# Rotary remainder products on half of the array's rows, an even and an odd key tile side by side, with three score banks

## The chip, the cores and the metric

The kernel runs on one core of one Trainium2 chip. The metric is device time in microseconds, the median of three runs. The profiled execution is a single run with its own time.

## The reference

One transformer layer over 2048 tokens of width 512. The part that matters here is the latent attention with 16 heads, a query of 128 plain and 64 rotary dimensions per head, and one rotary key that all heads share:

```python
cq = rms_norm(x @ w_qa.T, q_a_ln_w)
q = (cq @ w_qb.T)                       # 16 heads x (128 plain + 64 rotary)
ckv = x @ w_kva.T                       # 128 latent + 64 rotary
k_pe = rotate(ckv[..., 128:])           # one rotary key for all heads
ckv_l = rms_norm(ckv[..., :128], kv_a_ln_w)
scores = (q_nope . k_nope + q_pe . k_pe) * scale, causal mask, softmax
out = softmax @ v, then @ w_o.T
x1 = layernorm(x + out);  result = layernorm(x1 + x1 @ (w * s).T + bias)
```

Everything is float32. The kernel folds the key and value up-projections into the queries and into the output projection, so keys and values are both the 128-wide latent row of a token (plus the 64 rotary dimensions for the scores).

## The kernel before, in words

Three phases stand one behind the other, and each engine's instructions are in a fixed order.

The prepare phase (up to about 160 us) projects the tokens, turns the results so that the feature dimension lies on partitions, and writes each as two fp32r tensors, a rounded part ("hi") and the remainder ("lo"). `token_places` (line 412) names the places. The rotary key has 64 dimensions; its rotated row is made twice, so that `key_pe` holds the same 64 rows on partitions 0 to 63 and on 64 to 127, with a hi part (index 0) and a lo part (index 1). `lo(t)` (line 508) makes the lo parts on the vector engine.

The attention phase (about 160 to 1725 us) runs over 64 iterations: 4 groups of 4 heads, and in each the 16 query tiles of 128 tokens, two by two (a pair `s` is two iterations). Iteration `it` works on query tile `tile_of(it)` and takes that number plus one key tiles; there are 544 (iteration, key tile) steps in all. `key_tile(it, t)` (line 603) says which key tile step `t` takes: the diagonal one first, then 0, 1, 2 and so on. For each step:

- `scores` (line 1146) does five matmuls of 128 rows and 512 columns (4 heads by 128 queries) into one PSUM bank: hi key by hi query, hi key by lo query, lo key by hi query for the latent part, then two for the rotary part. `q_pe` holds the hi part of the rotary query on partitions 0 to 63 and its lo part on 64 to 127, so the fourth matmul (hi rotary key on both halves) gives both hi by hi and hi by lo, and the fifth (lo rotary key on both halves) gives lo by hi and lo by lo.
- the scalar engine copies the bank into a ring of 24 slots (`copy_scores`, line 1265), the vector engine keeps the running maximum (`max_of`, line 1426; `masked`, line 1414, for the diagonal tile), and that frees the bank: there are two banks for scores, `N_SCORES = 2`.
- six or more steps later come: subtract the maximum (vector), exp (scalar), rounding to hi (scalar), remainder (GpSimd), the running sum (vector), and `values` (line 1187), three matmuls of 512 columns.

Other work of the tensor engine stands between them: the projection of the queries (`project_q`, `project_pe`), turning and spreading of maxima and sums (`turn_max`, `spread_max`, `turn_sum`, `spread_sum`), and the output projection (`project_out`). Six kinds of these share a set of three auxiliary banks, `N_AUX = 3`: a use waits (`shared`, line 1108) until the reader of the use three before it is done.

The order of all this is written by `plan` (line 817) from a `timetable` (line 658) of slots and phases, with `waits_for` (line 721) saying what must stand ahead of a step. The reader of a use (for `spread_sum` it is `normalise` and the two halves of the output rounding) is put into phase `READ` of the next slot, unless an auxiliary bank is wanted earlier. The phases of a slot are, in order, SPREAD, SCORES_AT, COPIES, SHIFT, EXP, ROUND, VALUES, READ, MAX, USE_AT.

The rotary part of the queries goes through DRAM to change its layout: `store_pe` writes it, and `load_pe` (line 1049) fetches it with four DMAs on SyncE's queue into `q_pe`, one for each of (hi, lo) by (first, second half of the 64 dimensions). The first score step of a pair waits for them ahead of its fourth matmul.

The last phase (from about 1725 us) is the feed-forward layer; the change does not touch it. On the tensor engine the preparation begins with 16 transposes of 128 rows (line 302) and 4 of 64 rows (line 304):

```python
for k in range(KH):
    for o in range(4):
        pe.transpose(m.bank[k][...], wa_rows[:, o, k * P:k * P + P], m.ident[:, :])
for k in range(KH):
    mm = pe.transpose(m.bank[4][...], wa_tail[0:DR, k * P:k * P + P], m.ident[0:DR, 0:DR])
mm.then_inc(wa_turned, 1)
```

Of the kernel before, what the change touches and what calls it, by code (L numbers as in the profile page):

```python
# [8 lines left out]
F32R = mybir.dt.float32r  # L9
BF16 = mybir.dt.bfloat16  # L10
ALU = mybir.AluOpType
# [3 lines left out]
P = 128  # L15
S = 2048
# [4 lines left out]
DN, DR, DV = 128, 64, 128  # L21
DQ = DN + DR
HALF = DR // 2
# [7 lines left out]
HG = H // G  # L31
# [7 lines left out]
def chunk(c):  # L39

    return (c + 1) % NCH


def stored(view):

    return view.bitcast(F32)
# [7 lines left out]
class Memory:  # L54


    def __init__(self, nc, ctx):
        def sb(name, shape, dt=F32):
            return ctx.enter_context(nc.sbuf_tensor(name, shape, dt))

        self.bank = [ctx.enter_context(nc.psum_tensor(f"bank{n}", [P, 512], F32)) for n in range(4, 8)]

        self.rows = ctx.enter_context(nc.psum_tensor("rows", [P, 4 * 512], F32))
        self.bank = [self.rows[:, 512 * n:512 * n + 512] for n in range(4)] + [b[:, :] for b in self.bank]

        self.key_c = sb("key_c", [P, 2, S], F32R)
        self.key_pe = sb("key_pe", [P, 2, S], F32R)
        self.val = sb("val", [P, 2, NT, C], F32R)
        self.cq = sb("cq", [P, 2, KR, 512], F32R)
        self.wq = sb("wq", [P, 2, KR, WCOL], F32R)  # L70
        self.wo = sb("wo", [P, 2, HG, HID], F32R)
        self.ident = sb("ident", [P, P])
        self.ident16 = sb("ident16", [P, P], BF16)
        self.mask16 = sb("mask16", [P, P], BF16)
        self.table = sb("table", [P, 2, 4 * P])
        self.small = sb("small", [P, 64])

        self.pool = sb("pool", [P, RING * 512])

        self.cq_dram = nc.dram_tensor("cq_dram", (NCH, P, 2 * KR * 512), F32, kind="Internal").ap()  # L80
        self.wq_dram = nc.dram_tensor("wq_dram", (G, P, 2 * KR * WCOL), F32, kind="Internal").ap()
        self.wo_dram = nc.dram_tensor("wo_dram", (G, P, 2 * HG * HID), F32, kind="Internal").ap()

        self.turned_tables = self.pool[:, 0:8 * P].rearrange("p (w n) -> p w n", n=P)
        self.table_dram = nc.dram_tensor("table_dram", (4, P, 8, P), F32, kind="Internal").ap()
        self.pe_dram = nc.dram_tensor("pe_dram", (G * NT // 2, 2, 2, P, 2 * P), F32, kind="Internal").ap()
        self.table_copied = ctx.enter_context(nc.semaphore("table_copied"))
        self.table_stored = ctx.enter_context(nc.semaphore("table_stored"))
        self.y_stored = ctx.enter_context(nc.semaphore("y_stored"))

        self.wo_free = ctx.enter_context(nc.semaphore("wo_free"))
        self.cq_free = ctx.enter_context(nc.semaphore("cq_free"))

        self.ffn_w_loaded = ctx.enter_context(nc.semaphore("ffn_w_loaded"))
        self.y_first_loaded = ctx.enter_context(nc.semaphore("y_first_loaded"))
        self.y_dram = nc.dram_tensor("y_dram", (NT, P, HID), F32, kind="Internal").ap()


def prepare_phase(nc, m, x, w_qa, w_kva, w_qb, w_kvb, w_o, q_ln, kv_ln, ident_in, mask_in, cos_in, sin_in):
# [6 lines left out]
    with ExitStack() as ctx:  # L106
# [3 lines left out]
        at = 0  # L110
# [56 lines left out]
        tok_lo = sem("tok_lo")  # L167
# [244 lines left out]
        def token_places(c, t):  # L412

            yield (TR[:, 0:QLR].rearrange("p (k n) -> p k n", k=KR), lambda a: m.cq[:, a, :, t * P:t * P + P], None)
            yield TR[:, QLR:QLR + C], lambda a: m.key_c[:, a, bass.ds(chunk(c) * 512 + t * P, P)], kv_w
            yield KT, lambda a: m.key_pe[:, a, bass.ds(chunk(c) * 512 + t * P, P)], None

        @block.scalar
        def _(act):
# [67 lines left out]
        def _(dve):  # L487
# [12 lines left out]
            with dve.Fori(0, NCH) as c:  # L500
# [7 lines left out]
                def lo(t):  # L508

                    for n, (src, dst, scale) in enumerate(token_places(c, t)):  # L510
                        dve.wait_ge(tok_hi, c * 12 + 3 * t + max(n, 1) + 1)
                        if scale is None:
                            nc.vector.tensor_tensor(dst(1), src, stored(dst(0)), ALU.subtract).then_inc(tok_lo, 1)
                        else:
                            nc.vector.scalar_tensor_tensor(out=dst(1), in0=src, scalar=scale, in1=stored(dst(0)),
                                                           op0=ALU.mult, op1=ALU.subtract).then_inc(tok_lo, 1)
# [43 lines left out]
N_TILE = G * NT * (NT + 1) // 2  # L560
N_PAIR = N_ITER // 2
LEAD = 6
N_SCORES, N_AUX = 2, 3
Y_FIRST = 10


# [23 lines left out]
def tile_of(it):  # L590

    return 2 * pair_of(it // 2) + 1 - it % 2
# [5 lines left out]
def keys(it):  # L598

    return tile_of(it) + 1  # L600


def key_tile(it, t):

    return tile_of(it) if t == 0 else t - 1


FIRST = [sum(keys(n) for n in range(it)) for it in range(N_ITER + 1)]
# [3 lines left out]
def number(it, t):  # L612

    return FIRST[it] + t
# [95 lines left out]
def previous(it, t, back):  # L710

    n = number(it, t) - back
    return TILES[n] if n >= 0 else None
# [7 lines left out]
def waits_for(step):  # L721

    what, it, *rest = step
    if what == "scores":
# [2 lines left out]
            yield ("q_lo", it // 2, j)  # L727
        if number(it, *rest) >= N_SCORES:
            yield ("max", *previous(it, *rest, N_SCORES))
    elif what == "max":  # L730
        yield ("scores", it, *rest)
        if number(it, *rest) >= RING:
# [84 lines left out]
def plan():  # L817

    order, given, uses = [], set(), []

    def give(step):

        if step in given:
            return
        given.add(step)
        for before in waits_for(step):
            give(before)
        if step[0] in AUX_USES:
            if len(uses) >= N_AUX:
                for reader in readers(uses[-N_AUX]):  # L830
                    give(reader)
            uses.append(step)
        order.append(step)

    at = {}
    for n, phase, step in timetable():
        at.setdefault((n, phase), []).append(step)
        for reader in readers(step):
            at.setdefault((n + 1, READ), []).append(reader)
    for key in sorted(at):  # L840
        for step in at[key]:
            give(step)
    return order, uses
# [25 lines left out]
def attention_phase(nc, m, w_ffn, scale_w):  # L869


    with ExitStack() as ctx:
        def sb(name, shape, dt=F32):
            return ctx.enter_context(nc.sbuf_tensor(name, shape, dt))
# [4 lines left out]
        ring = m.pool[:, :].rearrange("p (r n) -> p r n", r=RING)  # L879
        q_c = sb("q_c", [P, 2, HG, 512], F32R)  # L880
        q_pe = sb("q_pe", [P, HG, 512], F32R)
        split_p = sb("split_p", [P, 2, 2, 512], F32R)
        o_t = sb("o_t", [P, 2, 512], F32R)
        o_sum = sb("o_sum", [P, 2, 512])
# [60 lines left out]
        def by_head(view):  # L945

            return view.rearrange("p (h n) -> p h n", h=HG)
# [21 lines left out]
        def q_slot(it):  # L969

            return (it // 2 % 2) * 2 * P + tile_of(it) % 2 * P
# [17 lines left out]
        def _(sp):  # L989
# [59 lines left out]
            def load_pe(s):  # L1049
                at = pair_slot(s)  # L1050
                sp.wait_ge(pe_stored, 32 * (s + 1))
                if s:
                    sp.wait_ge(pe_loaded, 64 * s)
                if s >= 2:

                    sp.wait_ge(scores_ready, finished(2 * s - 3))
                for x in range(2):
                    for e in range(2):
                        row = DR * x + HALF * e
                        sp.dma_start(stored(q_pe[row:row + HALF, :, at:at + 2 * P]),  # L1060
                                     m.pe_dram[s, x, e].rearrange("(h d) n -> d h n", h=HG)).then_inc(pe_loaded, 16)
                if s == 1:
                    store_tables()
                if s == 2:
                    sp.wait_ge(m.table_stored, 64)
                if MADE <= s + 2 < N_PAIR:
                    load_table(s + 2)
# [24 lines left out]
        def _(pe):  # L1092
# [53 lines left out]
            def scores(it, t):  # L1146
                n, j, at = number(it, t), key_tile(it, t), q_slot(it)
                if t == 0:

                    if it % 2 == 0:  # L1150
                        pe.wait_ge(q_lo, q_count(it // 2, PAIRS - 1))
                if n >= N_SCORES:

                    pe.wait_ge(scores_maxed, n - N_SCORES + 1)
                out = SCORES[n % N_SCORES]
                k_c, k_pe = m.key_c[:, :, j * P:j * P + P], m.key_pe[:, :, j * P:j * P + P]
                terms = [(k_c[:, 0], q_c[:, 0, :, at:at + P]), (k_c[:, 0], q_c[:, 1, :, at:at + P]),
                         (k_c[:, 1], q_c[:, 0, :, at:at + P]), (k_pe[:, 0], q_pe[:, :, at:at + P]),
                         (k_pe[:, 1], q_pe[:, :, at:at + P])]
                for z, (k, q) in enumerate(terms):  # L1160
                    if z == 3 and t == 0 and it % 2 == 0:
                        pe.wait_ge(pe_loaded, 64 * (it // 2 + 1))
                    mm = pe.matmul(by_head(out), k, q, start=(z == 0), stop=(z == 4))  # L1163
                mm.then_inc(scores_ready, 1)

            def turn_max(it):
                u = ("turn_max", it)
# [619 lines left out]
```

## Time and profile before

| | |
|---|---|
| median of 3 runs | 1812.79 us (1812.04 to 1815.03) |
| the profiled execution | 1809.61 us, of which the span of its instructions is 1807.6 us |
| tensor engine, matmuls | 1704.4 us busy, 94% |
| tensor engine, weight loads | 1391.9 us busy, 77% |
| vector engine | 1401.4 us, 78% |
| scalar engine | 1095.1 us, 61% |
| GpSimd | 972.5 us, 54% |
| DMA | 94 GB/s on average |

Busy time is the union of an engine's instructions. A matmul's duration in the trace contains the time until its last results are through, and the next begins before that; so the distance from start to start says what a matmul occupies, not its duration. A weight load overlaps the matmul ahead of it. "Idle before" is time in which the engine did nothing ahead of an instruction, and the name behind the arrow is what ended it.

### The profile page before, as it was taken

Reading aid. Unit: us, or ns where it says so; the run is one execution under the profiler, and the core shown is the slowest. Engines: PE = TensorE matmul, PEld = TensorE weight load, DVE = VectorE, ACT = ScalarE, POOL = GpSimd, SP = SyncE. Lnnn points to the kernel's source line nnn. Section 1 sums busy time; section 2 is a strip of 40 time slices with the busy share of each in tenths; the row PEclk is TensorE's granted clock in tenths of the full one; section 3 lists DMA queues with packets and bytes.
Section 4 is the critical chain, followed back from the end, with each engine's and each line's share of the span. In section 5 each row is a group of like instructions: output and inputs, shape, how many; then the busy total and the mean of one; then the engine's idle time right before and its main releaser. Section 6 shows DMA issues by size and latency. Waiting matters only on the chain. (4 is left out here: it accounts for less than half of the span.)

```text
span 1807.6 us, 27750 instructions
## 1 busy us (share of the span) xinstructions
PE 1704.4 (94%) x8729; PEld 1391.9 (77%) x8729; DVE 1401.4 (78%) x2531; ACT 1095.1 (61%) x2088; POOL 972.5 (54%) x883
## 2 busy tenths in 40 slices
PE   5997899999999899999999999999999999998586
PEld 3665778888888788888888788888888888886432
DVE  1555578888888688888888688888888888888376
ACT  2553367667666567676666576766667766676310
POOL 2321245556555456655555455655655666566555
PEclk9998999999999999999999999999999999999899
DMA  7785412112322221213231322212222211111411
GB/s 241 280 328 224 131 58 82 59 60 76 117 71 82 88 88 38 81 58 117 71 99 36 123 65 77 65 59 98 66 71 88 65 59 59 56 45 30 141 63 58
DMA packets 109960, 170.52 MB, mean 94 GB/s; under 512 B 12992, under 2 KB 83648, under 8 KB 107456
## 3 DMA queue, kind: packets, MB, share of 16 engines
q1 hardware_dynamic: 100992, 121.14, 21.1%
q0 software_dynamic: 7104, 23.60, 4.0%
q10 hardware_dynamic: 1728, 24.12, 3.2%
q8 instruction: 67, 1.10, 0.3%
q14 instruction: 69, 0.57, 0.1%
HBM read 104.86 MB, written 68.16 MB: 96 GB/s over the span
## 5 line engine op out<-in xcount | busy, mean ns | idle before, releaser
L1342 POOL TENSOR_TENSOR split_p<-pool,split_p 128x512 fp32r<-128x512 f32 x544 | 702.6, 1294 | 509.6 <-ACT split_p L1287 509.3
L1163 PE MATMUL rows<-q_c,key_c 128*128 128x512 f32 x1632 | 475.9, 400 | 2.8 <-DVE top L1433 1.6
L1275 ACT COPY pool<-rows 128x512 f32<-128x512 f32 x480 | 281.8, 587 | 236.6 <-PE rows L1163 235.8
L1433 DVE TENSOR_TENSOR top<-rows,top 128x512 f32<-128x512 f32 x420 | 288.8, 688 | 137.4 <-ACT pool L1275 134.3
L1448 DVE TENSOR_TENSOR pool<-bank,pool 128x512 f32<-128x512 f32 x544 | 369.8, 680 | 20.5 <-PE bank L1183 20.5
L1280 ACT ACTIVATE pool<-pool 128x512 f32<-128x512 f32 x544 | 346.0, 636 | 16.0 <-DVE pool L1448 15.2
L1287 ACT CAST split_p<-pool 128x512 fp32r<-128x512 f32 x544 | 333.3, 613 | 14.8 <-PE bank L1196 14.8
L1163 PE MATMUL rows<-q_pe,key_pe 128*128 128x512 f32 x1088 | 337.0, 391 | 3.2 <-DMA q_pe<-pe_dram 3.2
L1460 DVE TENSOR_TENSOR bank<-bank,pool 128x512 f32<-128x512 f32 x480 | 331.0, 690 | 0.1
L1163 PEld LDWEIGHTS rows<-q_c,key_c 128*128 128x128 f32 x1632 | 288.9, 189 | 50.1 <-DVE top L1433 3.1
L1163 PEld LDWEIGHTS rows<-q_pe,key_pe 128*128 128x128 f32 x1088 | 204.2, 188 | 48.8 <-DMA q_pe<-pe_dram 3.6
L1196 PE MATMUL bank<-split_p,val 128*128 128x512 f32 x544 | 214.0, 393 | 5.0 <-POOL split_p L1342 4.7
L1193 PE MATMUL bank<-split_p,val 128*128 128x512 f32 x544 | 214.2, 394 | 3.1 <-ACT o_sum L1293 2.9
L1194 PE MATMUL bank<-split_p,val 128*128 128x512 f32 x544 | 212.2, 390 | 0.0
L1226 PE MATMUL rows<-wo,o_t 128*128 128x512 f32 x528 | 131.2, 398 | 9.6 <-issue 8.7
L1347 POOL TENSOR_TENSOR o_t<-o_sum,o_t 128x512 fp32r<-128x512 f32 x64 | 83.0, 1296 | 84.2 <-ACT o_t L1305 83.9
L1196 PEld LDWEIGHTS bank<-split_p,val 128*128 128x128 f32 x544 | 102.1, 188 | 32.9 <-POOL split_p L1342 11.4
L1226 PEld LDWEIGHTS rows<-wo,o_t 128*128 128x128 f32 x528 | 101.5, 193 | 32.6 <-issue 11.1
L1193 PEld LDWEIGHTS bank<-split_p,val 128*128 128x128 f32 x544 | 102.1, 188 | 28.5 <-ACT o_sum L1293 5.6
L1194 PEld LDWEIGHTS bank<-split_p,val 128*128 128x128 f32 x544 | 102.2, 188 | 21.2
L1305 ACT CAST o_t<-o_sum 128x512 fp32r<-128x512 f32 x64 | 39.7, 620 | 119.8 <-DVE o_sum L1472 94.0
L1128 PE MATMUL rows<-cq,wq 128*128 128x256 f32 x792 | 104.9, 287 | 0.0
(158 smaller groups left out, 2066.2 us busy)
## 6 DMA issues: line engine op xcount, KB each, us to landing
cq<-cq_dram SPq DMA_DIRECT2D x30, 768.0 KB, 5.0
y<-y_dram SPq DMA_DIRECT2D x64, 256.0 KB, 3.0
q_pe<-pe_dram SPq DMA_DIRECT2D x128, 128.0 KB, 2.7
y_dram<-y SPq DMA_DIRECT2D x64, 256.0 KB, 2.0
wq_dram<-wq ACTq DMA_DIRECT2D x4, 2304.0 KB, 11.7
wo_dram<-wo ACTq DMA_DIRECT2D x4, 2048.0 KB, 10.5
pe_dram<-by_sin SPq DMA_DIRECT2D x32, 256.0 KB, 2.1
pe_dram<-by_cos SPq DMA_DIRECT2D x32, 256.0 KB, 2.2
```

The lines of the kernel that those rows point to most:

```text
L1163: mm = pe.matmul(by_head(out), k, q, start=(z == 0), stop=(z == 4))
L1193: pe.matmul(OUT, m.val[:, 0, j, :], split_p[:, n % 2, 0, :], start=(t == 0), stop=False)
L1194: pe.matmul(OUT, m.val[:, 1, j, :], split_p[:, n % 2, 0, :], start=False, stop=False)
L1196: pe.matmul(OUT, m.val[:, 0, j, :], split_p[:, n % 2, 1, :], start=False, stop=(t == keys(it) - 1)).then_inc(values_done, 1)
L1226: mm = pe.matmul(aux(u), o_t[:, a, h * P:h * P + P], m.wo[:, b, h, :], start=(n == 0), stop=(n == 3 * HG - 1))
L1275: nc.scalar.copy(slot(n), SCORES[n % N_SCORES]).then_inc(scores_copied, 1)
L1280: nc.scalar.activation(slot(n), slot(n), ACT.Exp).then_inc(exp_done, 1)
L1287: nc.scalar.copy(split_p[:, n % 2, 0, :], slot(n)).then_inc(p_hi, 1)
L1342: nc.gpsimd.tensor_tensor(split_p[:, n % 2, 1, :], slot(n), stored(split_p[:, n % 2, 0, :]), ALU.subtract).then_inc(p_lo, 1)
L1433: nc.vector.tensor_tensor(out, SCORES[n % N_SCORES], slot(number(it, 0)) if t == 1 else out, ALU.max).then_inc(scores_maxed, 1)
L1448: nc.vector.tensor_tensor(slot(n), MAXES, slot(n), ALU.add).then_inc(shifted, 1)
L1460: nc.vector.tensor_tensor(TOTAL, TOTAL, slot(n), ALU.add).then_inc(summed, 1)
```

## The change

The lo part of the rotary key is no longer held twice. A new tensor `key_pe_lo` of half the width holds even key tiles on partitions 0 to 63 and odd ones on 64 to 127. The fifth matmul of a score step now has 64 rows: lo key by hi query, without the lo by lo product. Odd key tiles need the hi query on partitions 64 to 127, in a new tensor `q_pe_hi` that `load_pe` fills with two more DMAs.

Key tiles are taken in an order in which an even and an odd one follow each other. The first step of such a couple "opens" it: it does its four matmuls of 128 rows, its own 64-row matmul, and directly behind that the 64-row matmul of its partner, as the first product in the partner's bank. The partner, one step later, adds its four matmuls of 128 rows. Query tiles with an even number take their diagonal tile alone. There are three score banks and two auxiliary ones, and `normalise` stands in phase EXP of its slot in place of READ.

```diff
-        self.key_pe = sb("key_pe", [P, 2, S], F32R)
+        self.key_pe = sb("key_pe", [P, S], F32R)
+        self.key_pe_lo = sb("key_pe_lo", [P, S // 2], F32R)
...
-            yield KT, lambda a: m.key_pe[:, a, bass.ds(chunk(c) * 512 + t * P, P)], None
+            yield KT, lambda a: m.key_pe[:, bass.ds(chunk(c) * 512 + t * P, P)], None
...
+                        if n == 2:
+                            rows = slice(DR * (t % 2), DR * (t % 2) + DR)
+                            nc.vector.tensor_tensor(m.key_pe_lo[rows, bass.ds(chunk(c) * 2 * P + t // 2 * P, P)], src[rows],
+                                                    stored(dst(0))[rows], ALU.subtract).then_inc(tok_lo, 1)
...
-N_SCORES, N_AUX = 2, 3
+N_SCORES, N_AUX = 3, 2
...
-    return tile_of(it) if t == 0 else t - 1
+    i = tile_of(it)
+    if t < 1 + i % 2:
+        return i - t
+    return t - 1 - i % 2
+def opens_couple(it, t):
+    return (tile_of(it) + t) % 2 == 1 and t + 1 < keys(it)
+def closes_couple(it, t):
+    return t > 0 and opens_couple(it, t - 1)
...
+        if opens_couple(it, *rest) and number(it, *rest) >= N_SCORES - 1:
+            yield ("max", *previous(it, *rest, N_SCORES - 1))
...
-            at.setdefault((n + 1, READ), []).append(reader)
+            at.setdefault((n + 1, EXP if reader[0] == "normalise" else READ), []).append(reader)
...
-                    sp.wait_ge(pe_loaded, 64 * s)
+                    sp.wait_ge(pe_loaded, 96 * s)
...
+                for e in range(2):
+                    row = DR + HALF * e
+                    sp.dma_start(stored(q_pe_hi[row:row + HALF, :, at:at + 2 * P]),
+                                 m.pe_dram[s, 0, e].rearrange("(h d) n -> d h n", h=HG)).then_inc(pe_loaded, 16)
...
-                if n >= N_SCORES:
+                if n >= N_SCORES and not closes_couple(it, t):
                     pe.wait_ge(scores_maxed, n - N_SCORES + 1)
...
+                if closes_couple(it, t):
+                    for z, (k, q) in enumerate(whole):
+                        mm = pe.matmul(by_head(out), k, q, start=False, stop=(z == 3))
+                    mm.then_inc(scores_ready, 1)
+                    return
+                for z, (k, q) in enumerate(whole):
                     if z == 3 and t == 0 and it % 2 == 0:
-                        pe.wait_ge(pe_loaded, 64 * (it // 2 + 1))
-                    mm = pe.matmul(by_head(out), k, q, start=(z == 0), stop=(z == 4))
-                mm.then_inc(scores_ready, 1)
+                        pe.wait_ge(pe_loaded, 96 * (it // 2 + 1))
+                    pe.matmul(by_head(out), k, q, start=(z == 0), stop=False)
+                half_row(it, t, start=False, stop=True).then_inc(scores_ready, 1)
+                if opens_couple(it, t):
+                    if n + 1 >= N_SCORES:
+                        pe.wait_ge(scores_maxed, n + 1 - N_SCORES + 1)
+                    half_row(it, t + 1, start=True, stop=False)
+            def half_row(it, t, start, stop):
+                j, at = key_tile(it, t), q_slot(it)
+                rows = slice(DR * (j % 2), DR * (j % 2) + DR)
+                q = q_pe_hi if j % 2 else q_pe
+                return pe.matmul(by_head(SCORES[number(it, t) % N_SCORES]), m.key_pe_lo[rows, j // 2 * P:j // 2 * P + P],
+                                 q[rows, :, at:at + P], start=start, stop=stop)
```

## Rows read from the trace of the kernel before

**Rows 1.** Stages by windows: window, length, then each engine's busy us, clock, DMA

```profile
core 0: us, PE busy (x) PEld busy (x) DVE busy (x) ACT busy (x) POOL busy (x), PEclk, DMA share, GB/s
500.00:700.00 200.00, 195.32 (x1027) 165.89 (x1026) 161.46 (x274) 128.85 (x240) 111.88 (x91) 0.98 0.25 80
700.00:900.00 200.00, 199.73 (x1054) 170.10 (x1053) 168.62 (x284) 134.37 (x250) 116.59 (x94) 1.00 0.24 77
900.00:1100.00 200.00, 195.11 (x1027) 165.22 (x1026) 161.58 (x275) 129.77 (x242) 112.87 (x93) 0.99 0.23 75
```

**Rows 2.** Waits of the weight loads, 190 to 1725 us: total us, times, longest

```profile
PEld bank L1196 <- POOL split_p L1342: 11.4, 16, 1.1
...
PEld bank L1193 <- ACT o_sum L1293: 5.6, 7, 1.3
...
PEld rows L1163 <- DVE top L1433: 3.1, 4, 1.6
```

**Rows 3.** Groups by line and form: shapes, count, busy us, mean ns, idle before

```profile
L1163 PE MATMUL rows<-q_c,key_c 128*128 128x512 f32 x1632 | 475.9, 400 | 2.8 <-DVE top L1433 1.6 <-DVE pool L1422 1.2
L1163 PE MATMUL rows<-q_pe,key_pe 128*128 128x512 f32 x1088 | 337.0, 391 | 3.2 <-DMA q_pe<-pe_dram 3.2
```

**Rows 4.** Timeline of matmuls around 906 us: start us, us, engine, line, count

```profile
905.98 0.39 PE L1193 MATMUL bank<-split_p,val 128*128 128x512 f32 x1
906.20 0.39 PE L1194 MATMUL bank<-split_p,val 128*128 128x512 f32 x1
906.43 0.39 PE L1196 MATMUL bank<-split_p,val 128*128 128x512 f32 x1
906.66 0.84 PE L1163 MATMUL rows<-q_c,key_c 128*128 128x512 f32 x3
907.34 0.62 PE L1163 MATMUL rows<-q_pe,key_pe 128*128 128x512 f32 x2
```

**Rows 5.** Timeline of the weight loads of the same stretch

```profile
905.98 0.19 PEld L1194 LDWEIGHTS bank<-split_p,val 128*128 128x128 f32 x1
906.21 0.19 PEld L1196 LDWEIGHTS bank<-split_p,val 128*128 128x128 f32 x1
```

**Rows 6.** Timeline of the vector engine, one step and the next

```profile
907.08 0.68 DVE L1433 TENSOR_TENSOR top<-rows,top 128x512 f32<-128x512 f32 x1
907.67 0.68 DVE L1448 TENSOR_TENSOR pool<-bank,pool 128x512 f32<-128x512 f32 x1
908.27 0.69 DVE L1460 TENSOR_TENSOR bank<-bank,pool 128x512 f32<-128x512 f32 x1
908.87 0.68 DVE L1433 TENSOR_TENSOR top<-rows,top 128x512 f32<-128x512 f32 x1
```

**Rows 7.** Durations at line 1163 (rotary part), ns min/median/max, first and last start

```profile
L1163 PE MATMUL rows<-q_pe,key_pe x1088: 387/389/497, 184.4 to 1644.9; 128*128 128x512 f32 x182
```

**Rows 8.** Timeline of matmuls at the start: from 128-row to 64-row transposes

```profile
18.35 1.27 PE L302 MATMUL rows<-ident,wa_rows 128*128 128x128 f32 x5
19.55 0.69 PE L304 MATMUL bank<-ident,wa_tail 64*128 64x64 f32 x4
```

**Rows 9.** Timeline of the weight loads of the same stretch

```profile
18.99 0.23 PEld L302 LDWEIGHTS rows<-ident,wa_rows 128*128 128x128 f32 x1
19.55 0.39 PEld L304 LDWEIGHTS bank<-ident,wa_tail 64*128 64x128 f32 x3 [0.33 <-issue]
```

**Rows 10.** Durations of the matmuls at line 302

```profile
L302 PE MATMUL rows<-ident,wa_rows x16: 421/421/474, 15.9 to 19.2; 128*128 128x128 f32 x16
```

**Rows 11.** Timeline: four 128-column transposes later in the kernel

```profile
908.47 0.60 PE L1212 MATMUL rows<-ident,sums 128*128 128x128 f32 x4
```

**Rows 12.** The rotary queries' loads: durations of the issue, and when they were waited for

```profile
L1060 SPq DMA_DIRECT2D q_pe<-pe_dram x128: 303/432/1684, 177.8 to 1619.2; - x128
...
195.22 0.73 PE L1163 MATMUL rows<-q_pe,key_pe 128*128 128x512 f32 x2 [3.17 <-DMA q_pe<-pe_dram]
```

More of the change, by code:

```diff
@@ L511, in lo @@
                         dve.wait_ge(tok_hi, c * 12 + 3 * t + max(n, 1) + 1)
-                        if scale is None:
+                        if n == 2:
+                            rows = slice(DR * (t % 2), DR * (t % 2) + DR)
+                            nc.vector.tensor_tensor(m.key_pe_lo[rows, bass.ds(chunk(c) * 2 * P + t // 2 * P, P)], src[rows],
+                                                    stored(dst(0))[rows], ALU.subtract).then_inc(tok_lo, 1)
+                        elif scale is None:
                             nc.vector.tensor_tensor(dst(1), src, stored(dst(0)), ALU.subtract).then_inc(tok_lo, 1)
@@ L881, in attention_phase @@
         q_pe = sb("q_pe", [P, HG, 512], F32R)
+        q_pe_hi = sb("q_pe_hi", [P, HG, 512], F32R)
         split_p = sb("split_p", [P, 2, 2, 512], F32R)
@@ L1151, in scores @@
                         pe.wait_ge(q_lo, q_count(it // 2, PAIRS - 1))
-                if n >= N_SCORES:
+                if n >= N_SCORES and not closes_couple(it, t):
                     pe.wait_ge(scores_maxed, n - N_SCORES + 1)
                 out = SCORES[n % N_SCORES]
[L1156 to L1159, printed above, removed]
@@ L1160, in scores @@
-                for z, (k, q) in enumerate(terms):
-                    if z == 3 and t == 0 and it % 2 == 0:
-                        pe.wait_ge(pe_loaded, 64 * (it // 2 + 1))
-                    mm = pe.matmul(by_head(out), k, q, start=(z == 0), stop=(z == 4))
-                mm.then_inc(scores_ready, 1)
+                k_c, k_pe = m.key_c[:, :, j * P:j * P + P], m.key_pe[:, j * P:j * P + P]
+                whole = [(k_c[:, 0], q_c[:, 0, :, at:at + P]), (k_c[:, 0], q_c[:, 1, :, at:at + P]),
+                         (k_c[:, 1], q_c[:, 0, :, at:at + P]), (k_pe, q_pe[:, :, at:at + P])]
```

## The prediction

> **What bounds the kernel now.** I read the stages first. In the attention phase the matmuls are busy for 195 to 200 of every 200 us and the granted clock is 0.98 to 1.00, the upper of its two levels, 2.4 GHz; the vector engine stands at 161 to 169 us, the others lower [rows 1]. So the tensor engine is the bound, and the question is what each of its instructions occupies. For that I don't take the durations (400 and 391 ns, [rows 3]), which overlap, but the distance from start to start in the timeline: 905.98, 906.20, 906.43, 906.66, which is 0.227 us for a matmul of 512 columns, and 0.227 again for the three latent score matmuls (906.66 to 907.34, three in 0.68) [rows 4]. Each weight load begins when the matmul ahead of it begins (905.98 and 906.21 beside 905.98 and 906.20) [rows 4, 5], so its time is covered. The waits confirm that little else holds the tensor engine: from 190 to 1725 us the three longest causes that this change could touch are 11.4 us for GpSimd's remainders, 5.6 us for the copy of the output and 3.1 us for the maximum that frees a score bank [rows 2].
>
> A step costs eight such matmuls, 8 x 0.227 = 1.816 us. The vector engine needs three operations for it, at 907.08, 907.67, 908.27 and the next step's at 908.87: 1.79 us [rows 6]. In a stretch of plain steps it is thus only 0.03 us behind; projections and transposes on the tensor engine, which have less vector work, give it its slack.
>
> **What goes, at best.** Nothing goes from the count: 544 steps keep eight matmuls, of which 544 get 64 rows. A query tile i has i + 1 keys; an odd i gives (i + 1)/2 couples (36 over the eight odd tiles of a group), an even i gives i/2 (28) and its diagonal tile alone (8). Times four groups that is 256 couples and 32 single 64-row matmuls. If the two of a couple really run at the same time, each couple saves one matmul: 256 x 0.227 = 58.1 us.
>
> **What the two loads of a couple cost.** An fp32r matmul whose weights were not loaded beforehand lasts 497 ns in place of 389 [rows 7]: an uncovered load is 108 ns. If the partner's load can only follow the first one's and neither is covered, the partner starts 0.108 later and the couple occupies 0.227 + 0.108; the saving is 256 x (0.227 - 0.108) = 30.5 us. With both covered behind the fourth matmul (2 x 0.108 = 0.216 against 0.227) it is the full 58.1. I take 30.5, because the next point uncovers the loads.
>
> **What a change between 128 and 64 rows costs.** Before, there is none in attention. There is exactly one change between the two back to back in the whole trace, and no semaphore stands between its sides: line 302 to line 304. The five last 128-row transposes span 1.27 us with a last duration of 0.421 [rows 8, 10], so they start (1.27 - 0.421)/4 = 0.212 apart, the last one at 18.35 + 0.85 = 19.20, and its successor was due at 19.41. Its weight load would have begun at 19.20, as every load in [rows 5] begins with the matmul ahead. It begins at 19.55, after 0.33 us with no load under way, put down to "issue", that is to nothing that the profile shows [rows 9]. That is 0.14 us after the last 128-row matmul had taken in its columns: the array was emptied before it was loaded for 64 rows. So a change costs (a) a rest D until the array is empty and (b) a load that nothing covers.
>
> D at the attention's clock has to be estimated from two ends. The transposes at 18.35 start 0.212 apart where four of the same form later fit into 0.60 in all, at most 0.15 apart [rows 8, 11], so they ran at the lower level, 1.2 GHz. If D scales with the clock it is 0.07 us, if it doesn't it is 0.14. The part of a matmul's duration beyond its start-to-start distance is 421 - 212 = 209 ns there [rows 8, 10] and 389 - 227 = 162 ns in attention [rows 4, 7], a ratio of 0.78, which gives 0.14 x 0.78 = 0.11. I take 0.10, between that and the scaled end. One change is then 0.10 + 0.108 = 0.21 us, with ends 0.07 + 0.108 = 0.18 and 0.14 + 0.108 = 0.25. That the way back to 128 rows costs the same is not in the trace; its lower end is zero, and I take the same price, since the array has to be empty and newly loaded there too.
>
> The Trainium skill, page "TensorEngine Tiling (Array Packing)", section "Tiling Modes", says that changing the tiling mode, as opposed to the tile, drains the engine; by that rule, with the row's price, the sum comes out as below, and the one change that the trace has agrees with it. The page "TensorE: Matmul & The Clock Gate", part 3, speaks the other way: it has tiles of different rows start about 4 ns apart, which by itself would give 256 x (0.227 - 0.004) = 57 us of saving; no row here shows two tiles together.
>
> There are 256 + 32 = 288 excursions to 64 rows and back, 576 changes: 576 x 0.21 = 121 us, ends 576 x 0.18 = 104 and 576 x 0.25 = 144 us. All lies on the engine that is the bound.
>
> **The banks and the order.** A third score bank takes away at most the 3.1 us of waits for a maximum [rows 2]. The opener adds a wait between its two 64-row matmuls, for the maximum of two steps before; behind it on the tensor engine stand the partner's product and all later work, in front of it for the vector engine only what it has to do anyway. With couples that maximum belongs to the opener of the couple before, whose scores were ready about 11 matmuls (2.5 us) earlier; one scalar copy and one vector operation of 0.68 [rows 6] fit in. I cost it at nothing; without that cover each would cost some tenths of a us. Two auxiliary banks in place of three: going through the order of the kernel before, 345 of the 352 uses have the reader of the use two before them already ahead of them, mostly with three or more tensor steps between; the other 7 would wait for a vector operation pulled forward, at most two to three operations of 0.68, 2 us. Between 0 and 14 us; I take 3, near the low end, because long projections stand between most of them. The early `normalise` moves one operation of 0.68 past one `sum` on the vector queue: the scalar engine's copy and the output projection behind it come sooner, the sum 0.6 us later; nothing on the tensor engine's queue waits for either at once. Zero.
>
> **The loads.** Two more DMAs for each of 32 pairs, 64 x 0.43 us of issue on SyncE's queue [rows 12]. They pass the next y and table loads, which wait in turn for later work. The tensor engine waited for these loads only in the first pairs (3.17 us at 195.22) [rows 12], where two more issues add about 0.9 us: 1 us in all. The remainder of the key in the prepare phase is one operation on 64 partitions in place of 128: zero.
>
> **The sum.** -30.5 (couples) + 121 (changes) + 3 - 3 (banks) + 1 (loads) = +91.5. A slower tensor engine absorbs part of the waits for GpSimd and the scalar engine, 17 us in [rows 2], since those come relatively sooner: I take 12 off. +80 us, so 1809.6 + 80 = 1890 for a profiled execution; the median of the runs shown lies 3.2 above the profiled one, which gives **1893 us**. With 104 and 144 for the changes: 1876 and 1916.
>
> **The rivals.** (1) *Half price*: only one of the two directions costs a change, 288 x 0.21 = 60: -30.5 + 60 + 1 - 6 = +25, 1838 us; the trace shows only one direction, and that is what speaks for it. (2) *No change cost in fp32r matmuls at full clock, the two run side by side*: -58.1 on the tensor engine. A couple then takes 15 matmuls, 3.405 us, 1.70 per step, and the vector engine with 1.79 becomes the bound in plain stretches [rows 6]; it catches up in the projections, so I let 50 us through: 1763. If the second load stays uncovered, -30: 1783. For it: the loads would be covered, the banks differ, nothing else in the order forbids it; against it: the load of line 304, which did wait [rows 9]. (3) *It doesn't do what it says*: 64-row matmuls run one after the other and switching is free: 0 + 1 + 3 - 3, 1814 us. Rival 2 is the one that ends on the faster side; its place is the change ahead of and behind each couple, and it decides from a price of (0.227 x 256)/576 = 0.10 us for one change downwards, or 30.5/576 = 0.05 where the second load is uncovered.
>
> **The chances.** Forecast 0.55; half price 0.13; side by side 0.27 (0.17 at 1763, 0.10 at 1783); no overlap and free changes 0.05. Faster by over 0.2% (which is about what a measurement of this kernel can tell from no change) 0.27, within 0.2% 0.04, slower 0.69. The range must reach from the slow ends nearly to the fast case to leave out no more than 2 in 10: 1760 to 1920. The forecast's own range is 1865 to 1920.
>
> **What would show it.** In the changed trace the load for `key_pe_lo` does not begin with the fourth matmul but some 0.3 us later, with "issue" before it; the first matmul of each couple lasts about 497 ns; the next 128-row matmul behind a couple starts 0.227 + 0.21 = 0.44 us after the partner's. The stages would show more idle weight-load time with the same clock, and in a plain stretch it is 14 x 0.227 + 0.335 + 0.42 = 3.9 us from opener to opener in place of 16 x 0.227 = 3.6. If instead the two 64-row matmuls start within 0.11 us of each other and the load of the next begins with them, rival 2 holds, and the vector engine's waits for scores shrink. If they start 0.227 apart with no gaps, rival 3. Wrong would be, above all, that the one change at 1.2 GHz between transposes tells nothing of fp32r matmuls at 2.4.

## The result and the profile after

The changed kernel takes 1875.93 us (median of 4 runs, 1872.96 to 1876.6) against 1812.47 us for the kernel before in 4 runs beside them: a ratio of 1.0349, 95% interval 1.0336 to 1.0361. That is 63 us or 3.5% slower, where 80 us slower was predicted (1893; range 1760 to 1920). The profiled execution's span is 1874.6 us, 67 more than before: 62.6 of them lie in the attention phase (1565.4 us in place of 1502.8 from its first latent score matmul to its last matmul of `values`), the rest ahead of it and behind it.

The stages come first, as in [rows 1]. Columns: window, its length, busy us of each engine with instructions, granted clock, DMA share, GB/s. Kernel after:

```profile
core 0: us, PE busy (x) PEld busy (x) DVE busy (x) ACT busy (x) POOL busy (x), PEclk, DMA share, GB/s
500.00:700.00 200.00, 194.83 (x988) 150.56 (x987) 153.94 (x258) 120.36 (x223) 104.07 (x86) 0.98 0.29 87
700.00:900.00 200.00, 199.65 (x1007) 153.53 (x1005) 166.77 (x276) 130.92 (x243) 114.26 (x93) 1.00 0.24 77
900.00:1100.00 200.00, 194.46 (x981) 150.09 (x980) 154.52 (x258) 122.81 (x227) 105.22 (x87) 0.98 0.28 84
```

The tensor engine is as busy as before and its clock is the same, but in 600 us it gets 2976 matmuls through in place of 3108 (988 + 1007 + 981 against 1027 + 1054 + 1027). Busy time alone would hide the whole loss. The weight loads are busy for 454 us in place of 501, in part because there are 4% fewer of them, in part because the two loads of a couple now lie on top of each other. What stopped them stands in their waits (total us, times, longest), kernel after, 190 to 1790 us:

```profile
PEld rows L1205 <- issue: 102.3, 286, 0.4
PEld bank L1235 <- issue: 38.9, 159, 0.2
PEld bank L1235 <- ACT split_p L1329: 30.0, 121, 0.5
...
PEld bank L1238 <- POOL split_p L1384: 9.5, 13, 1.1
PEld rows L1192 <- DMA q_pe_hi<-pe_dram: 5.3, 1, 5.3
```

Line 1205 is the 64-row matmul, line 1235 the first matmul of `values`, which stands behind it. 286 times the load ahead of a 64-row matmul was held by nothing that the profile shows ("issue"). Before, no load of the score matmuls had an entry of this kind; the longest waits were those of [rows 2]. Some holds of line 1235 are put down to the scalar engine (the wait for the rounded probabilities that the instruction also carries); the length of the hold is the same with either name, 0.24 us on average up to 1640 us (36.7 us for 150 and 27.5 us for 113), and in the run "64 rows in the kernel before" (below) nearly all holds of this line have "issue"; so that wait is not taken for their cause. The timeline has one couple, first the matmuls, then the loads (start us, us; answers to [rows 4] and [rows 5]). Kernel after:

```profile
907.30 0.39 PE L1192 MATMUL rows<-q_pe,key_pe 128*128 128x512 f32 x1
907.62 0.50 PE L1205 MATMUL rows<-q_pe,key_pe_lo 64*128 64x512 f32 x1
907.62 0.50 PE L1205 MATMUL rows<-q_pe_hi,key_pe_lo 64*128 64x512 f32 x1
908.05 0.50 PE L1235 MATMUL bank<-split_p,val 128*128 128x512 f32 x1
908.38 0.40 PE L1236 MATMUL bank<-split_p,val 128*128 128x512 f32 x1
```

```profile
907.62 0.18 PEld L1205 LDWEIGHTS rows<-q_pe,key_pe_lo 64*128 64x128 f32 x1 [0.35 <-issue]
907.62 0.18 PEld L1205 LDWEIGHTS rows<-q_pe_hi,key_pe_lo 64*128 64x128 f32 x1
908.04 0.19 PEld L1235 LDWEIGHTS bank<-split_p,val 128*128 128x128 f32 x1 [0.24 <-ACT split_p L1329]
908.15 0.19 PEld L1236 LDWEIGHTS bank<-split_p,val 128*128 128x128 f32 x1
```

The reader is to see four things. The two 64-row matmuls start together (3 ns apart, median over the 256 couples, worked out from their start times). Their two loads start together as well. Those loads begin 0.32 after the fourth matmul, not with it: 0.227 until it has taken in its columns, and 0.09 more. (That the array runs empty in these 0.09 is how the prediction read such a hold. The trace shows the hold alone, and the matmul's modelled end, 907.69, lies 0.07 behind the load's start.) A matmul whose load is not covered is recorded from the start of that load and lasts 0.50 in place of 0.39, so the real start is 907.73. And the load for the next 128-row matmul begins at 908.04: 907.73 + 0.227 = 907.95, and again 0.09 more, again with 0.108 of load behind it. In stretches of two score steps without other work of the tensor engine (89 in each kernel), the two take 3.83 us in place of 3.63 (medians): one matmul of 0.227 less and two changes of 0.20 more are +0.17 of these 0.20.

### The profile page after: what moved, and what is told of

It is laid out like the page before. It is cut to its first block and busy times, and to the rows that moved or that the text cites. A ratio compares the mean times of both kernels' runs of the same rounds, so it can differ in the third digit from the quotient of the medians.

```text
span 1874.6 us, 27814 instructions
## 1 busy us (share of the span) xinstructions
PE 1771.3 (94%) x8729; PEld 1326.2 (71%) x8729; DVE 1419.7 (76%) x2531; ACT 1096.0 (58%) x2088; POOL 971.1 (52%) x883
## 5 line engine op out<-in xcount | busy, mean ns | idle before, releaser
L1384 POOL TENSOR_TENSOR split_p<-pool,split_p 128x512 fp32r<-128x512 f32 x544 | 702.4, 1293 | 587.0 <-ACT split_p L1329 586.5
L1235 PE MATMUL bank<-split_p,val 128*128 128x512 f32 x544 | 244.1, 449 | 1.2 <-ACT o_sum L1335 1.0
L1238 PE MATMUL bank<-split_p,val 128*128 128x512 f32 x544 | 214.7, 395 | 4.1 <-POOL split_p L1384 3.8
L1236 PE MATMUL bank<-split_p,val 128*128 128x512 f32 x544 | 213.9, 393 | 0.0
L1235 PEld LDWEIGHTS bank<-split_p,val 128*128 128x128 f32 x544 | 101.7, 187 | 80.9 <-issue 38.9
L1205 PE MATMUL rows<-q_pe,key_pe_lo 64*128 64x512 f32 x288 | 143.5, 498 | 0.0
L1205 PE MATMUL rows<-q_pe_hi,key_pe_lo 64*128 64x512 f32 x256 | 127.4, 498 | 0.0
L1238 PEld LDWEIGHTS bank<-split_p,val 128*128 128x128 f32 x544 | 102.1, 188 | 32.2 <-POOL split_p L1384 9.5
L1268 PE MATMUL rows<-wo,o_t 128*128 128x512 f32 x492 | 118.7, 390 | 0.0
L1192 PE MATMUL rows<-q_pe,key_pe 128*128 128x512 f32 x288 | 113.0, 393 | 4.9 <-DMA q_pe_hi<-pe_dram 4.9
L1205 PEld LDWEIGHTS rows<-q_pe,key_pe_lo 64*128 64x128 f32 x288 | 52.7, 183 | 91.6 <-issue 91.6
```

What stands on the lines that cost most here:

```text
L1192: pe.matmul(by_head(out), k, q, start=(z == 0), stop=False)
L1205: return pe.matmul(by_head(SCORES[number(it, t) % N_SCORES]), m.key_pe_lo[rows, j // 2 * P:j // 2 * P + P], q[rows, :, at:at + P], start=s ...
L1235: pe.matmul(OUT, m.val[:, 0, j, :], split_p[:, n % 2, 0, :], start=(t == 0), stop=False)
L1238: pe.matmul(OUT, m.val[:, 0, j, :], split_p[:, n % 2, 1, :], start=False, stop=(t == keys(it) - 1)).then_inc(values_done, 1)
L1384: nc.gpsimd.tensor_tensor(split_p[:, n % 2, 1, :], slot(n), stored(split_p[:, n % 2, 0, :]), ALU.subtract).then_inc(p_lo, 1)
```

## The experiments

The question was whether the 63 us are 576 changes between 64 and 128 rows (theory A), the banks, order and early product (rival B), a pair that doesn't overlap (rival C), or a price for one direction only (rival D). Each result is the median and the ratio to the kernel before on the same chip, with its 95% interval; differences between two kernels are differences of ratios times 1812. The later theories and rivals, E to H, are told in the expectations. A line "-" of an edit is that of the kernel it was made from, which the text names.

**All on 128 rows again.** Made from the changed kernel. The key order, the opener's second product, the banks and the early normalise stay; `key_pe` has its lo part back, and `key_pe_lo`, `q_pe_hi` and its loads are gone (not shown).

```diff
-                rows = slice(DR * (j % 2), DR * (j % 2) + DR)
-                q = q_pe_hi if j % 2 else q_pe
-                return pe.matmul(by_head(SCORES[number(it, t) % N_SCORES]), m.key_pe_lo[rows, j // 2 * P:j // 2 * P + P],
+                rows, q = slice(0, P), q_pe
+                return pe.matmul(by_head(SCORES[number(it, t) % N_SCORES]), m.key_pe[rows, 1, j * P:j * P + P],
```

> The changed kernel with its order, its opener's extra product, its banks and its early normalise, but each fifth product on 128 rows again (no q_pe_hi and its two loads). Theory A (what the change costs are the 576 changes between 128 and 64 rows, 0.20 us each, and the two 64-row matmuls of a couple do overlap): 1812.5 plus only what banks and order cost, 5 us, so 1813 to 1821. Rival B (the cost lies in the banks, the order or the partner's early product): 1860 or more.

Measured: 1810.88 us, ratio 0.9998 (0.9988 to 1.0007). Rival B falls: everything but the rows (and the two loads for them) comes to nothing that can be told. It lies even under theory A's 1813 to 1821, which had 5 us for banks and order.

**Both of a couple on the same 64 rows.** Made from the kernel of the last run.

```diff
-                rows, q = slice(0, P), q_pe
+                rows, q = slice(0, DR), q_pe
```

> As couples_128rows, but each fifth product has 64 rows and both of a couple use partitions 0 to 63, so that they can't run side by side while the number of changes stays 576. Theory A: the overlap that the changed kernel has is worth 256 x 0.227 = 58 us, so 1876 + 58 = 1934 (1925 to 1940). Rival C (the 3 ns between the two starts in the trace is only how the profile writes them, and they run one after the other already): 1876.

Measured: 1925.82 us, 1.0633 (1.0616 to 1.0651), which is (1.0633 - 1.0349) x 1812 = 51 us above the changed kernel. The timeline of one couple in this kernel:

```profile
705.50 0.40 PE L1182 MATMUL rows<-q_pe,key_pe 128*128 128x512 f32 x1
705.83 0.73 PE L1194 MATMUL rows<-q_pe,key_pe 64*128 64x512 f32 x2
706.49 0.50 PE L1224 MATMUL bank<-split_p,val 128*128 128x512 f32 x1
```

From the first 64-row matmul to the next 128-row one are 0.66 us where the changed kernel has 908.05 - 907.62 = 0.43: the 0.23 of one matmul. The overlap is real, rival C falls. (Both pairs of numbers are also the medians over the 256 couples, 0.658 and 0.431.) The total shows 51 of the 58 us that 256 x 0.227 makes. In the profiled executions it is 53.5, and 55.8 in the attention phase alone (1621.2 against 1565.4). There the gaps of over 0.5 us between two starts of matmuls (what they have beyond 0.227) came to 2.3 us less, which makes up the 58; the stretches ahead of this phase and behind it are 2.3 us shorter, and the rest is spread between runs. The changes, against the same order on 128 rows, are (1.0633 - 0.9998) x 1812 = 115 us, 0.200 for each of 576, with all else in it that comes with 64 rows.

**64 rows in the kernel before.** One line of it, without couples or other banks:

```diff
-                         (k_pe[:, 1], q_pe[:, :, at:at + P])]
+                         (k_pe[0:DR, 1], q_pe[0:DR, :, at:at + P])]
```

> The kernel before, with nothing changed but the fifth product of each step: 64 rows (partitions 0 to 63) in place of 128, so the product of the two remainders is left out. No couples, two score banks, three auxiliary ones. Theory A: 544 excursions, 1088 changes of 0.20 us, +218 us less some waits that a slower tensor engine absorbs: 2030 (2000 to 2035). Rival B: 1812. Rival D (only the way into 64 rows costs): 1921.

Measured: 2021.98 us, 1.1169 (1.115 to 1.1188): 212 us, or 0.195 for each of 1088 changes. Less arithmetic in the fifth product makes the kernel 12% slower. Rival D's 1921 is far outside. The waits of this kernel's weight loads, 190 to 1640 us:

```profile
PEld rows L1163 <- issue: 169.2, 475, 0.4
PEld bank L1193 <- issue: 105.2, 429, 0.2
```

Here nothing but the row count differs from the kernel before, and the holds stand on both sides of the 64-row matmul: ahead of it (line 1163) and ahead of the first of `values` (line 1193).

**The singles back on 128 rows.** Made from the changed kernel.

```diff
                 q = q_pe_hi if j % 2 else q_pe
+                if not (opens_couple(it, t) or closes_couple(it, t)):
+                    rows, q = slice(0, P), q_pe
```

> The changed kernel, with the fifth product of the 32 diagonal tiles that have no partner on all 128 rows; rows 64 to 127 then multiply the odd tile's remainder with the query's remainder, a product of two remainders that does not belong there but is tiny. Theory A: 64 changes fewer at 0.20, 12.8 us less than the changed kernel: 1863. Rival B: 1876.

Measured: 1863.39 us, 1.0286 (1.0269 to 1.0303): (1.0349 - 1.0286) x 1812 = 11 us less than the changed kernel, for 64 changes fewer, 0.18 each. These 32 matmuls had no partner and could only lose; this is the better form of the change, and still 52 us slower than before.

**The couple's second product left out.** The fifth product of the second step of each couple is not computed, and the others have 128 rows as in the first run; the edit is shown against the changed kernel, without the lines that it shares with the first run.

```diff
-                if opens_couple(it, t):
-                    if n + 1 >= N_SCORES:
-                        pe.wait_ge(scores_maxed, n + 1 - N_SCORES + 1)
-                    half_row(it, t + 1, start=True, stop=False)
...
-                if n >= N_SCORES and not closes_couple(it, t):
+                if n >= N_SCORES:
...
-                        mm = pe.matmul(by_head(out), k, q, start=False, stop=(z == 3))
+                        mm = pe.matmul(by_head(out), k, q, start=(z == 0), stop=(z == 3))
```

> As couples_128rows, but the fifth product of each couple's second step is left out (the output then lacks the remainder of those keys' rotary part). 15 matmuls per couple and no change of rows: what the change would have been worth with free changes. If the tensor engine alone decides: 1811 - 58 = 1753. If the vector engine with its 1.79 us a step takes over in plain stretches, as rival 2 of the prediction has it: 1763 (1757 to 1770).

Measured: 1763.26 us, 0.9737 (0.9721 to 0.9753), 48 us faster. So free changes would have brought about 48 of the 58 us. Its stages:

```profile
500.00:700.00 200.00, 194.64 (x1032) 164.70 (x1032) 166.67 (x285) 132.46 (x248) 115.43 (x95) 0.99 0.24 76
700.00:900.00 200.00, 199.40 (x1065) 170.07 (x1064) 174.83 (x294) 138.71 (x258) 120.80 (x98) 1.00 0.26 86
900.00:1100.00 200.00, 194.39 (x1010) 163.90 (x1009) 166.19 (x281) 132.73 (x248) 115.45 (x94) 0.98 0.25 80
```

The vector engine rises to 166 to 175 us of 200, from 161 to 169 in [rows 1]. The total is the 1763 of rival 2, which let the vector engine with its 1.79 us a step take over from the tensor engine with 1.70. The trace doesn't bear that out: where two score steps stand without other work of the tensor engine (89 stretches), they take 3.43 us (median), which is 15 x 0.227 = 3.41 and not 2 x 1.79 = 3.58. The missing 10 us are spread. These waits of the weight loads rose most against the kernel with the same order on 128 rows; first couples_128rows, then this kernel, 190 to 1720 us:

```profile
PEld bank L1227 <- POOL split_p L1373: 9.5, 13, 1.1
PEld bank L1214 <- DVE pool L1479: 1.6, 2, 1.3
PEld bank L1224 <- ACT o_sum L1324: 1.5, 2, 0.8
```

```profile
PEld bank L1222 <- POOL split_p L1368: 13.1, 21, 1.1
PEld bank L1209 <- DVE pool L1474: 4.8, 12, 1.5
PEld bank L1219 <- ACT o_sum L1319: 4.5, 8, 0.8
```

That is 3 to 4 us more each for GpSimd, the vector and the scalar engine, 9.8 in all. That these are the missing 10 is argued from the size.

**Each pair twice in one stay at 64 rows.** Made from the changed kernel.

```diff
-                half_row(it, t, start=False, stop=True).then_inc(scores_ready, 1)
-                if opens_couple(it, t):
-                    if n + 1 >= N_SCORES:
-                        pe.wait_ge(scores_maxed, n + 1 - N_SCORES + 1)
-                    half_row(it, t + 1, start=True, stop=False)
+                if not opens_couple(it, t):
+                    half_row(it, t, start=False, stop=True).then_inc(scores_ready, 1)
+                    return
+                half_row(it, t, start=False, stop=False)
+                if n + 1 >= N_SCORES:
+                    pe.wait_ge(scores_maxed, n + 1 - N_SCORES + 1)
+                half_row(it, t + 1, start=True, stop=False)
+                half_row(it, t, start=False, stop=True).then_inc(scores_ready, 1)
+                half_row(it, t + 1, start=False, stop=False)
```

> The changed kernel, with each couple's two 64-row matmuls issued twice in one stay at 64 rows (the remainder products of couples are counted twice in the output). Theory A: a further pair in the same stay costs 0.227 and no change: 256 x 0.227 = 58 us above the changed kernel, 1933. Rival E (each 64-row pair pays an uncovered load of 0.108 also within a stay): 256 x 0.335 = 86, 1960. Rival C (no overlap): 256 x 0.454 = 116, 1991.

Measured: 1933.12 us, 1.0673 (1.0655 to 1.0691): (1.0673 - 1.0349) x 1812 = 59 us above the changed kernel. Matmuls and loads of one such couple:

```profile
904.50 0.40 PE L1192 MATMUL rows<-q_pe,key_pe 128*128 128x512 f32 x1
904.83 0.49 PE L1209 MATMUL rows<-q_pe,key_pe_lo 64*128 64x512 f32 x1
904.83 0.50 PE L1209 MATMUL rows<-q_pe_hi,key_pe_lo 64*128 64x512 f32 x1
905.16 0.39 PE L1209 MATMUL rows<-q_pe,key_pe_lo 64*128 64x512 f32 x1
905.16 0.39 PE L1209 MATMUL rows<-q_pe_hi,key_pe_lo 64*128 64x512 f32 x1
905.49 0.51 PE L1239 MATMUL bank<-split_p,val 128*128 128x512 f32 x1
```

```profile
904.82 0.18 PEld L1209 LDWEIGHTS rows<-q_pe,key_pe_lo 64*128 64x128 f32 x1 [0.37 <-issue]
904.83 0.18 PEld L1209 LDWEIGHTS rows<-q_pe_hi,key_pe_lo 64*128 64x128 f32 x1
904.93 0.19 PEld L1209 LDWEIGHTS rows<-q_pe,key_pe_lo 64*128 64x128 f32 x1
904.93 0.19 PEld L1209 LDWEIGHTS rows<-q_pe_hi,key_pe_lo 64*128 64x128 f32 x1
```

The second pair lasts 0.39 again: its loads at 904.93 are covered by the first pair (which really starts there), and four products need two matmuls' time. Rival E's 86 us for an uncovered load in each pair falls, and so do rival C's 116. A stay costs its two changes once, with one pair in it or two.

**The banks and the early normalise by themselves,** both in the kernel before.

```diff
-N_SCORES, N_AUX = 2, 3
+N_SCORES, N_AUX = 3, 2
```

> The kernel before with three score banks and two auxiliary ones, nothing else. couples_128rows came out equal to before, so either each of its parts is worth nothing or two cancel. Theory A: 1811 (1808 to 1814). Rival F (two auxiliary banks cost what the early normalise gives back): 1816 or more here.

Measured: 1817.74 us, 1.0032 (1.0018 to 1.0047): 6 us. Theory A's 1808 to 1814 was missed, and rival F's first half holds. Its weight loads wait for the normalise (line 1472), a wait that the kernel before doesn't have, while the one for the maximum falls from 3.1 us [rows 2] to 0.5. From 190 to 1640 us:

```profile
PEld bank L1128 <- DVE o_sum L1472: 3.7, 8, 0.7
...
PEld bank L1141 <- DVE o_sum L1472: 2.0, 2, 1.0
```

```diff
-            at.setdefault((n + 1, READ), []).append(reader)
+            at.setdefault((n + 1, EXP if reader[0] == "normalise" else READ), []).append(reader)
```

> The kernel before with normalise in phase EXP of its slot, nothing else. Theory A: 1811 (1808 to 1814). Rival F: 1806 or less here.

Measured: 1810.92 us, 0.9993 (0.9983 to 1.0002): no change that can be told, so rival F's second half, 1806 or less, fails. The two edits together in the kernel before:

> The kernel before with three score banks, two auxiliary ones and the early normalise, in one. Alone the banks gave +5.5 us and the early normalise -1.3. Theory G (the early normalise pays only where two auxiliary banks make the tensor engine wait for it, and that is why couples_128rows came out at no change): 1811 to 1814. Rival H (the two don't touch each other, and what made couples_128rows equal was the order of key tiles or the partner's early product): 1816 to 1818.

Measured: 1812.63 us, 1.0003 (0.9994 to 1.0013). Theory G's number holds, and rival H's 1816 to 1818 falls: the early normalise is worth some 5 us beside two auxiliary banks, and nothing that can be told beside three. By what way is shown only in part: the waits for the normalise fall from 5.7 to 4.6 us, and 2.1 us of waits for the scalar engine's copy of the output (line 1293) are gone. And in the changed kernel, with this line undone:

> The changed kernel with normalise back in phase READ. Theory G: the gain of the early place is 2 to 5 us, so 2 to 5 above the changed kernel: 1877 to 1880. Rival H: 1874 to 1876.

Measured: 1874.65 us, 1.0348 (1.0331 to 1.0365), the same as with it. Here theory G missed (1877 to 1880) and rival H's 1874 to 1876 came in: the late place costs nothing in the changed kernel. Up to 1640 us its weight loads wait 3.9 us for the normalise with either place.

## Why the prediction was right, and where its size was off

**The mechanism** was the one forecast. The one change of rows in the trace of before, between transposes at 1.2 GHz [rows 8, 9], told what 576 would do among fp32r matmuls at 2.4 GHz. (The granted clock of that stretch has no row: the profile's clock record begins at 28.7 us. But transposes of this form start 0.213 apart wherever it later records 1.2 GHz, and 0.109 apart at 2.4.) Most signs named for it appeared: the load 0.32 us behind the fourth matmul with "issue" before it, 0.50 for the first in each mode, 0.43 for the predicted 0.44 to the next 128-row matmul, the same clock. Two did not: the partner started 3 ns behind, where 0.11 was the mark of rival 2, and a plain couple took 3.83 us in place of 3.9. On this point rival 2 was right, on the changes the forecast.

**The price of a change** was right: 0.21 predicted, made of 0.10 + 0.108. In the trace it is 0.09 to get in and 0.096 to get out (medians over the couples) plus 0.108 each time, 0.20; the runs give 0.200 and 0.195. So 576 changes cost 116 us, not 121, and the assumption that both directions cost the same, for which no row existed, holds. The 0.14 us at 1.2 GHz stand beside 0.09 to 0.10 at 2.4: neither scaled with the clock (0.07) nor fixed; the ratio of the durations' tails gave 0.11. The two differ in the form of the matmuls too, so this is no rule for the clock. The Trainium skill's rule (page "TensorEngine Tiling (Array Packing)", section "Tiling Modes") is that a change of mode drains the engine; the holds of 0.09 us agree with it.

**The term that was mis-sized** is "what the two loads of a couple cost". I let the partner's load follow the first one's, 0.108 later, and took 30.5 us of saving. Both loads go in at once, 3 ns apart, and so do the matmuls: the saving is the full 58.1 us. That is 28 us of error. The Trainium skill, page "TensorE: Matmul & The Clock Gate", part 3, puts tiles of different rows about 4 ns apart; the trace agrees with 3 ns, and I had set that figure aside for want of a row.

**The absorbed waits** were the error the other way. I took off 12 us; nothing came off. Against the same order on 128 rows the gaps of over 0.5 us between two starts in the attention phase are not shorter (29.0 us beyond 0.227 each, in place of 27.5). The terms that are left, -58.1 + 116.1 = +58.0, are 5 us below what was measured. The loads' 1 us is part of them: the first pair's wait for them (weight loads) is 5.3 us, 4.4 in the kernel on 128 rows. Most of the rest is visible: between 190 and 1640 us, the start-to-start distances of 512-column matmuls that lie between 220 and 245 ns average 229.5 ns in place of 228.3, over some 3500 of them, 4 us. The kernels with 64 rows but without the loads of `q_pe_hi` show it too (229.4 with both on the same rows, 229.2 in the kernel before with 64 rows), the one on 128 rows does not (228.2). It isn't a matter of which matmuls are counted: from the second matmul of `values` to the third it is 231.2 in place of 227.7, while deep in an output projection both kernels stay within 0.2 of 226.7. So it belongs to the 64 rows and not to the loads; by what way stays open.

**The balance.** From the predicted 80: 28 less for the overlap, 5 less for the price of a change, 12 more for waits that were not absorbed, 4 to 5 more for the slower spacing make 63 to 64. So the number came out as near as it did in part because errors of both signs met, and that is luck.

**Banks and order** came out at zero as summed (+3 - 3), as a sum of two things that cancel: 6 us for the second auxiliary bank taken away, given back by the early normalise. The 3 us that I put on the auxiliary bank were half of that, and I had the early normalise at nothing. The opener's wait for a maximum came to 0.3 us in all (line 1205, up to 1640 us), as costed; in a plain stretch it stands 3.8 us behind the scores in question, not the 2.5 that I counted.

**The vector engine as the next bound** was worked out at 50 us let through of 58; the run without changes let 48 through. The number was right, the reason was not borne out: plain steps ran at the tensor engine's pace, and the 10 us were spread over waits for three engines.

**Whether any form of this wins.** A stay at 64 rows costs 2 x 0.20 = 0.40 us and a pair in it saves 0.227, so a stay pays from two pairs on, by 0.05 us. That needs four score banks, which leaves one auxiliary bank of the five that they share. Counting stays of at most two pairs over the 16 query tiles, with the singles on 128 rows, gives 36 in a group (20 for odd tiles, 16 for even ones), 144 in all: 144 x 0.40 = 58 us, against the 58 saved, before anything that one auxiliary bank costs. This is an estimate; it was not run. None of the kernels that ran and did the whole computation beats the one before.

## What to carry to other kernels

Compare the rows that a new matmul uses with those of its neighbours before counting what it saves: halving the rows of one product among full ones cost 0.39 us each, over one and a half times a whole matmul of 512 columns. Side by side on two halves of the array worked fully here, loads included, but a stay has to be long enough to pay for getting in and out; so gather such products, and leave one without a partner on all rows. When a step's price is disputed, look for a single instance of it anywhere in the trace, the start-up included; here one pair of lines outside the bound phase decided the sign.

## What the runs showed of the hardware

- Changing between 128 and 64 rows held the next load for 0.09 to 0.10 us after the last matmul had taken in its columns, and left the 0.108 us of that fp32r load uncovered, in each direction, at 2.4 GHz (medians over 256 couples). It also happens with the 64-row matmul at rows 0 to 63 and no partner (0.195 a change).
- Two 64-row matmuls of 512 columns on different halves of the rows, in different banks, ran in the time of one, their starts and those of their loads 3 ns apart; on the same half they took one matmul's 0.227 more.
- The profile put the hold down to "issue" (150 times ahead of line 1235) or, where the instruction also carries a wait, to the engine waited for (113 times), with the same 0.24 us either way.
- The start-to-start distance of other matmuls grew by 1.2 ns on average (228.3 to 229.5) where 64-row ones stood among them; the cause is open.
